# Order of the first layer's shifted copies, key groups and projection evictions, and of the last layer's normalization

## The reference

```python
x = x + _L0_conv_ref(_gn(x), ...)   # lambda layer: 4 heads, keys with softmax over positions, relative positions
x = x + _L1_conv_ref(_gn(x), ...)   # attention, 16 heads, half of them look back, half ahead
x = x + _L2_conv_ref(_gn(x), ...)   # attention with relative positions by height and width
x = x + _L3_conv_ref(_gn(x), ...)   # 3x3 filter shared by all channels, then a 1024x1024 product in tensor-train form, bias, relu
```

## Time and profile before

| | us |
|---|---|
| median of 3 runs | 1289.74 (1288.63 to 1292.06) |
| the profiled execution's own time | 1289.51 |
| its span, first to last instruction | 1287.5 |
| PE busy in the span | 1256.3 (98%) |
| DVE, ACT, POOL busy | 631.2, 537.7, 641.0 |

### The profile page before, as it was taken

The page is one execution under the profiler, slowest core; times in us unless marked ns, Lnnn a source line. Parts: engine busy times, 40 slices in busy tenths (PEclk is TensorE's granted clock), DMA queues, the critical chain, the costliest instruction groups (busy, mean ns, idle before and its releaser), DMA issues.

```text
span 1287.5 us, 19996 instructions
## 1 busy us (share of the span) xinstructions
PE 1256.3 (98%) x7216; PEld 1018.3 (79%) x7216; DVE 631.2 (49%) x1323; ACT 537.7 (42%) x1357; POOL 641.0 (50%) x726
## 2 busy tenths in 40 slices
PE   6999998999999999999999999999999999999998
PEld 4887894478888888888888888888888887778787
DVE  7533453774444233545243465754436656666212
ACT  3612140045656430656452066564305665543212
POOL 4633299055454556555546655455565554564000
PEclk9999999999999999999999999999999999999999
DMA  5211123022222233222233323233333233220011
GB/s 179 86 44 42 43 55 103 8 70 75 67 82 67 81 80 95 74 75 75 74 81 97 97 81 95 80 90 86 91 91 93 82 93 81 73 74 1 17 50 66
DMA packets 83297, 96.33 MB, mean 75 GB/s; under 512 B 24960, under 2 KB 46112, under 8 KB 83200
## 3 DMA queue, kind: packets, MB, share of 16 engines
q1 hardware_dynamic: 82048, 92.97, 25.4%
q10 hardware_dynamic: 1152, 2.10, 0.5%
HBM read 82.45 MB, written 8.39 MB: 71 GB/s over the span
## 4 chain that ended last, share of the span: by engine, by line
PE 88%; DVE 5%; issue 2%; ACT 2%; SPq 1%; DMA 0%; POOL 0%; ACTq 0%; DVEq 0%; POOLq 0%
PE PS L1126 53%; PE PS L680 6%; PE PS L1762 5%; PE PS L1194 4%; PE PS L1171 4%; PE PS L945 3%; PE PS L1210 2%; PE PS L960 2%; PE PS L1220 2%; PE PS L1779 2%; PE PS L1240 1%; SPq L1027 1%; PE PS L663 1%; PE PS L954 1%; PE PS L1186 1%
## 5 line engine op out<-in xcount | busy, mean ns | idle before, releaser
L1126 PE MATMUL PS<-XB,w_hi 128*128 128x512 f32 x1024 | 358.3, 403 | 1.4 <-POOL w_lo L227 1.2
L225 POOL CAST w_hi<-w_raw 128x512 fp32r<-128x512 f32 x195 | 124.9, 640 | 327.6 <-PE PS L1126 254.8
L227 POOL TENSOR_TENSOR w_lo<-w_raw,w_hi 128x512 fp32r<-128x512 f32 x195 | 253.7, 1301 | 15.6
L1126 PEld LDWEIGHTS PS<-XB,w_hi 128*128 128x128 f32 x1024 | 192.3, 188 | 41.8 <-issue 2.4
L1126 PE MATMUL PS<-XB,w_lo 128*128 128x512 f32 x512 | 200.0, 391 | 0.0
L1126 PE MATMUL PS<-XB,part 128*128 128x512 f32 x768 | 198.9, 397 | 0.0
L1126 PEld LDWEIGHTS PS<-XB,part 128*128 128x128 f32 x768 | 140.1, 188 | 27.8
L1404 ACT ACTIVATE part<-PS,nmax 128x256 f32<-128x256 f32 (+1 forms) x256 | 112.4, 447 | 64.4 <-DVE nmax L1529 44.7
L1421 ACT ACTIVATE part<-PS 128x384 f32<-128x384 f32 (+1 forms) x128 | 69.6, 544 | 135.1 <-PE PS L1194 134.9
L225 POOL CAST part<-part 128x512 fp32r<-128x512 f32 x85 | 55.8, 656 | 122.3 <-PE PS L1126 121.6
L227 POOL TENSOR_TENSOR part<-part,part 128x512 fp32r<-128x512 f32 x85 | 111.2, 1308 | 6.8
(11 more groups left out here) (140 smaller groups left out, 1986.4 us busy)
## 6 DMA issues: line engine op xcount, KB each, us to landing
w_raw<-in_w SPq DMA_DIRECT2D x187, 256.0 KB, 2.7
part<-in_w SPq DMA_DIRECT2D x85, 256.0 KB, 2.7
strips<-part SPq DMA_DIRECT2D x16, 256.0 KB, 3.3
out_x<-xT SPq DMA_DIRECT2D x16, 256.0 KB, 2.1
part<-strips SPq DMA_DIRECT2D x128, 24.0 KB
xT<-in_x ACTq DMA_DIRECT2D x8, 256.0 KB, 7.6
xT<-in_x SPq DMA_DIRECT2D x8, 256.0 KB, 9.8
w_raw<-in_w SPq DMA_DIRECT2D x16, 128.0 KB, 3.4
```

The costliest lines, as they stand in the source:

```text
L225: pool.tensor_copy(hi, raw).then_inc(w_hi_done, 1)
L227: pool.tensor_tensor(lo, raw, hi.bitcast(F32), ALU.subtract).then_inc(w_ready, 1)
L1126: m = nc.tensor.matmul(PS[:, bank, :], wt[:, (c % 4) * P:(c % 4) * P + P], rhs(hl, c), start=c == k == 0, stop=c == CK - 1 and k == 2)
```

## The change

Three edits of order and one of queue. ACT evicts the first two of the four query blocks ahead of `in_between`. The K groups are taken for half 1 of images 0 and 1 first, then half 0 of both, then image 2 and later image 3 with half 1 first; PE, DVE and the waits of Y follow that order. The 8 shifting DMAs of band 0 are issued by ACT, behind its last window copies, and SP issues bands 3, 1 and 2. In the last layer ACT and DVE normalize chunks 0 to 2, do the evictions of banks 0 and 1 of product 0, chunks 3 to 5, the evictions of banks 2 and 3, and chunks 6 and 7; and each chunk's hi and lo follow its own `norm.y`, where before `norm.y` of the next chunk came between.

```diff
-        def evac_q(jp):
-            for k in range(4):
+        def evac_q(jp, some):
+            for k in some:
...
                 exp_k(b)
+            evac_q(jp, range(2))
             if jp:
                 in_between()
-            evac_q(jp)
+            evac_q(jp, range(2, 4))
...
-    for kind, b in ("K", 0), ("K", 1), ("K", 2), ("Y", 0), ("K", 3), ("Y", 1), ("Y", 2), ("Y", 3):
-        add_groups(kind, b)
+    def add_keys_groups(b, mc):
+        groups.extend(("K", (b, mc, nh)) for nh in range(2))
...
+    KEYS = [(0, 1), (1, 1), (0, 0), (1, 0), (2, 1), (2, 0)]
+    for b, mc in KEYS:
+        add_keys_groups(b, mc)
+    add_y_groups(0)
+    for mc in (1, 0):
+        add_keys_groups(3, mc)
+    for b in range(1, B):
+        add_y_groups(b)
...
+    def shift(eng, t):
+        evacuated(eng, max(i for i, (kind, d) in enumerate(groups) if kind == "G" and d[0] == t))
+        for src, y, dst, mc in shifts(t):
+            eng.dma_start(A2[dst, mc, y, :, :].rearrange("p x g -> p (x g)"), G[t][src, y - rows_of[t][0], :])\
+                .then_inc(shifted[t], 16)
...
-                    evacuated(pe, at_group["K", (b, 1, 1)])
+                    evacuated(pe, at_group["K", (b, 0, 1)])
...
     def lambda_act(act):
         copy_windows(act, range(2, len(quads)))
+        shift(act, 0)
...
-        for t in rows_of:
-            evacuated(sp, ...)
-            for src, y, dst, mc in shifts(t):
-                sp.dma_start(...).then_inc(shifted[t], 16)
+        for t in (3, 1, 2):
+            shift(sp, t)
...
     def last_act(act):
-        for c in range(CK):
-            norm.y(nc.scalar, 5, c)
-            if c:
-                norm.head(5, c - 1)
-        norm.head(5, CK - 1)
+        def normalize(chunks):
+            for c in chunks:
+                norm.y(nc.scalar, 5, c)
+                norm.head(5, c)
+
+        normalize(range(0, 3))
...
+                if b == 0:
+                    normalize(range(3, 6) if tt == 0 else range(6, CK))
...
     def last_dve(dve):
+        def normalize(chunks):
+            for c in chunks:
+                norm.y(nc.vector, 5, c)
+                norm.rest(5, c)
+
+        normalize(range(0, 3))
...
+                if b == 0 and half:
+                    normalize(range(3, 6) if tt == 0 else range(6, CK))
```

More of the change, by code:

```diff
@@ L856, in later_layers, with add_y_groups @@
             groups.append(("G", (t, x, wide)))
[L858 to L861, removed]
-    for kind, b in ("K", 0), ("K", 1), ("K", 2), ("Y", 0), ("K", 3), ("Y", 1), ("Y", 2), ("Y", 3):
-        add_groups(kind, b)
+    def add_keys_groups(b, mc):
+        groups.extend(("K", (b, mc, nh)) for nh in range(2))
+    def add_y_groups(b):
+        groups.extend(("Y", (b, nh, vt)) for nh in range(2) for vt in range(2))
+    KEYS = [(0, 1), (1, 1), (0, 0), (1, 0), (2, 1), (2, 0)]
[6 more added lines that the diff above has]
+        add_y_groups(b)
     at_group = {group: i for i, group in enumerate(groups)}
@@ L948, in lambda_pe @@
                 b, mc, nh = d
-                if b == mc == nh == 0:
+                if (b, mc, nh) == (0, 1, 0):
                     pe.wait_ge(k_soft, B)
@@ L966, in lambda_dve, with add_keys @@
         read_g()
[L968 to L971, removed]
+        def add_keys(b, mc):
+            for nh in range(2):
+                add_shifted(b, mc, nh)
         def add_y(b, nh, vt):
@@ L984, in lambda_dve @@
         parts = [(nh, vt) for nh in range(2) for vt in range(2)]
-        for b in range(3):
-            add_keys(b)
+        for b, mc in KEYS:
+            add_keys(b, mc)
         for nh, vt in parts:
             add_y(0, nh, vt)
-        add_keys(3)
+        for mc in (1, 0):
+            add_keys(3, mc)
         for nh, vt in parts:
@@ L1023, in lambda_sp @@
         sp.dma_start(r2c[:, :], A["r2c"]).then_inc(cores_in, 16)
-        for t in rows_of:
-            evacuated(sp, max(i for i, (kind, d) in enumerate(groups) if kind == "G" and d[0] == t))
-            for src, y, dst, mc in shifts(t):
-                sp.dma_start(A2[dst, mc, y, :, :].rearrange("p x g -> p (x g)"), G[t][src, y - rows_of[t][0], :])\
-                    .then_inc(shifted[t], 16)
+        for t in (3, 1, 2):
+            shift(sp, t)
     def lambda_pool(pool):
```

## The result

The changed kernel takes 1278.68 us (median of 4 runs, 1278.25 to 1279.52) against 1289.83 on the same chip (4 runs, 1288.63 to 1292.06). The ratio is 0.9912, with a 95% interval of 0.9895 to 0.993. The forecast was 1278.9. The profiled execution took 1278.75, 10.76 less than that of before; its span is 1276.7.

The account below looks back on a forecast made before the run. PE carries 88% of the chain of waits, so its gaps and slow stretch counted. 1289.51 - 1.92 - 4.85 - 1.79 - 2.3 = 1278.65, plus 0.23 for the median: 1278.9 us; range 1277.3 to 1284.5.

Parts of the forecast that it names:

- Query evictions: PE's idle time before the transposes of query block 4 goes, as ACT evicts before copying windows: gain 1.92 us.
- The gap of the groups: PE's wait after 8 K groups for DVE's first add goes, as that add no longer needs band 0: gain 4.85 us.
- the clock: The 16 products behind the K groups' gap ran partly at half clock; without the gap that loss goes: gain 1.79 us.
- Margin: Ninth K group: its bank is free 0.56 us before PE arrives, less 0.3 us for two queues issuing together.
- The text on what would show it: Signs in the changed trace, among them DVE's first add starting within 1 us before PE's eighth K group ends.
- Two queues: SP's shifting copies beside ACT's eight DMAs: SP loses 0.3 us, bounded by nothing and 5.1 us, covered by the margin.
- The first rival: SP and ACT queues take turns issuing, so the groups' gap and half clock return: 1285.2 us, chance 0.09.
- The last layer: PE's gap before product 1 goes, as bank 0 is freed after three chunks of normalization: gain 2.3 us.
- The chunk's chain: Last layer's normalization: one chunk through DVE's `norm.y`, ACT's hi, DVE's lo and hand-overs takes 3.1 us, against 2.8 before.
- Rivals 3 and 4: Half clock from this kind of K group, 1280.7 us, chance 0.04; ACT's queue landing late, slower than before, chance 0.02.
- Rival 4: ACT's band 0 copies land late and hold up the fifth add; 28 us would give 1293 us; chance 0.02.

Follow-up runs that it names:

- e1: The kernel before with only the two query evictions moved ahead of the window copies: 1287.4 us, ratio 0.9977.
- e2: The kernel before with only the groups' edit (new order of the K groups, band 0 on ACT's queue): 1283.51 us, ratio 0.9942.
- e5: The changed kernel with the old order of the key groups, band 0 staying on ACT's queue: 1278.38 us, ratio 0.991.
- e9: The changed kernel with the last layer's normalization in one part, all 8 chunks ahead of the first evictions, new order within a chunk kept: 1282.96 us, ratio 0.994.
- e11: The changed kernel with the last layer's normalization in two parts, chunks 0 to 2 and 3 to 7: 1278.14 us, ratio 0.9907.
- e12: The changed kernel once more, unaltered, on the chip of the last four experiments: 1278.18 us, ratio 0.9907.
- e7: The changed kernel with 6 of band 0's copies issued by SP in the middle of band 2, the rest by ACT: 1283.03 us.
- e3: The kernel before with only the last layer's normalization in three parts: 1287.47 us, ratio 0.9972.
- e10: The changed kernel without the edit of the groups (query evictions and last layer edits only): 1285.8 us, ratio 0.9964.
- e4: The changed kernel with band 0's 8 copies back on SP behind band 2, new order of the key groups kept: 1278.35 us, ratio 0.9903.
- e8: The changed kernel with all 8 copies of band 0 on SP ahead of band 2's last eight, none on ACT: 1284.06 us.

## Why the prediction was right, point by point

- *Query evictions*, 1.92 expected, 1.94 found; e1 shows that it stands alone.
- *The gap of the groups*, 4.85, and *the clock*, 1.79: 6.64 expected, 6.65 found between the same two rows. Margin 0.56 less 0.3 expected, 0.39 found here and 0.22 to 0.96 over the seven traces without a gap. The text on what would show it asked for the first add within 1 us before the eighth K group ends; its own sum gives 212.39 - 210.73 = 1.66, and found is 210.80 - 209.31 = 1.49.
- *Two queues*, 0.3 us expected by the rows of the start, 0.3 found, and that match is luck: 0.2 of it is one issue, and the same count gives 0.02 to 0.05 us in e2, e5, e9, e11 and e12, which have the same two queues. The first rival, queues that take turns, would have had steps of 1.2 us on SP: shown wrong. The Trainium skill (Perfetto Trace Analysis, "DMA Instruction — HWDGE (DVE, Sync)") has both sequencers lock one generator in turn; the trace does not contradict a lock. But with both queues at work each had an issue out every 0.65 to 0.67 us, so by my estimate from these steps an issue can hold the generator for 0.33 us at most, about half of its 0.6; how long it does hold it, no run shows.
- *The last layer*, 2.3 expected, 2.51 found. I took product 0's length from its row less an overlap (21.8) and left out that product 1 itself ran 0.12 longer behind the gap.
- *The chunk's chain*, 3.1 us expected with POOL busy, 2.83 and 2.85 found (the ends of DVE's L418 at 1170.97, 1173.80 and 1176.65). The terms were off both ways: `norm.y` on DVE took 1.15 us against 0.93, the lo half 1.00 against 1.49. Bank 0 was free seven us early and not five. Banks 2 and 3, which I had reckoned free at product 0's end, came 2.1 us behind it, since ACT had to wait for it; that is still nine us before PE wants them.
- *Rivals 3 and 4*, the clock by kind of group and a late ACT queue: e2 shows the one wrong, and the fifth add of the changed kernel, which had nothing to wait for, the other. (Rival 4's 28 us would have given 1293.8, not 1293.)

Three points of the text did not hold, though they moved the sum little. First, "the clock fell behind the long gap, while the gaps of 1.79 and 2.19 are followed by products at their usual pace": true of the one execution, and not of the kernel. The gap of 2.2 us had the slow stretch behind it in e1 and e2, that of 2.6 in e7 and e9; only those of 1.8 and 1.9 never had it here. So the last layer's edit also takes away a loss of 0 or 1.7 us, which I gave it at nothing. Second, the clock's term has more than one size: 1.8 in the execution that I read, 2.2 in e3, 2.9 in e1 and 3.0 in e10. That the forecast came within 0.3 us is partly luck: three of the four runs of before beside the changed kernel were like the profiled one. Beside e1 to e4 the median of before was 1291.41, and against that one the step would have been some 13. Third, I priced the order of the keys and the ACT queue as one edit and did not ask which was needed. The rows would have told: with the old order and band 0 on ACT, the first add waits for band 2 just the same.

## What to carry to other kernels

Where an engine in order waits for several transfers, ask for each edit alone what the first wait then ends on: two edits that both take the last transfer out of the way look like a pair and are one gain. A chain ahead of a bank's release can be cut at any point that leaves the release early, and here two parts did as well as three. Price a gap of TensorE of two us or more with the clock behind it, as a chance, and look at the spread of the runs and at more than one trace before calling a gap cheap or a margin of tenths safe.

## What the runs showed of the hardware that was not expected

The half clock behind a gap comes or stays away in one and the same kernel. In these traces gaps of 1.8 and 1.9 us were not followed by it (four traces); that of 2.2 in two traces of three; 2.6 and 4.0 to 4.7 in all seven. The slow stretch was 3.4 or 6.8 us long and cost 1.7 to 3.0. Which of the two it was went with the place of its start. In e1, e3 and e10 the clock fell inside the gap of the groups, 1.1, 2.5 and 1.0 us before PE went on; the stretch was 6.8 us long and cost 2.9, 2.2 and 3.0. In the six other cases (the groups of before, e7 and e8, the last layer of e1, e2 and e9) it fell 0 to 1.3 us after PE had gone on, and was 3.4 us long. That holds for these nine stretches; what decides the place, no run here tests.

The runs of the kernel before fall into two heaps: of 31 runs beside the experiments 18 lie between 1288.4 and 1290.5 at a granted clock of 0.997 to 0.998, 13 between 1291.1 and 1292.7 at 0.995 to 0.996. The traces of e1, where a run at 0.995 has 6.8 and 3.4 us of half clock, show what the upper heap may be made of; no trace of before from that heap was taken, so for it this is an inference. The changed kernel has one heap, 1277.9 to 1279.5 in eight runs, and its gain is 11 us against the one heap and some 14 against the other.

SP's issues of copies inside the core take 0.59 us each whatever their size (16 to 128 KB), so the 53 in a row before were 35 us of one engine. In each of the 14 traces one of these issues, between 186 and 195 us, took 1.0 to 1.7 us (1.61 before, 1.42 in the changed kernel). Why is open, but the waits behind it go with it: the gap of the groups was 4.2 us in e1 and e10, where it took 1.1 and 1.0, and 4.6 and 4.7 in e3 and before, where it took 1.5 and 1.6; the margin without a gap was 0.96 in e12 at 1.2 us and 0.22 in e11 at 1.7. A margin of 0.56 us read from one trace is of the size of this scatter.
